# One-core convolution-attention kernel: the bias summed from two weighted records, block differences ahead of the statistics

## The reference

```python
qkv = jnp.einsum('bhwc,cd->bhwd', x, W_qkv)          # x here is _gn(x)
q, k, v = jnp.split(qkv, 3, axis=-1)                 # each turned to (b, c, n), n = h*w
k = jax.nn.softmax(k, axis=-1)
context = jnp.einsum('bdn,ben->bde', k, v)
out = jnp.einsum('bde,bdn->ben', context, q)         # back to (b, h, w, c)
return jnp.einsum('bhwc,cd->bhwd', out, W_out) + b_out
...
x = x + _L0_conv_ref(_gn(x), L0_conv_W_qkv, L0_conv_W_out, L0_conv_b_out)
```

## Time and profile before

| what | value |
|---|---|
| median of 3 runs | 1212.08 us (1211.97 to 1212.63) |
| the profiled execution | 1211.11 us, of which the span from first to last instruction is 1209.4 us |
| mean granted TensorE clock | 0.997 |
| TensorE matmuls, weight loads | 97% and 91% of the span |
| VectorE, ScalarE, GpSimd | 78%, 69%, 51% |
| DMA | 221 GB/s, 63% of the engines' time |

### The profile page before, as it was taken

The page is one execution under the profiler, slowest core; times in us unless marked ns, Lnnn a source line. Parts: engine busy times, 40 slices in busy tenths (PEclk is TensorE's granted clock), DMA queues, the critical chain, the costliest instruction groups (busy, mean ns, idle before and its releaser), DMA issues.

```text
span 1209.4 us, 21532 instructions
## 1 busy us (share of the span) xinstructions
PE 1174.3 (97%) x8270; PEld 1098.7 (91%) x8270; DVE 946.0 (78%) x1992; ACT 839.3 (69%) x1146; POOL 620.9 (51%) x289
## 2 busy tenths in 40 slices
PE   4989999999999999999999999999999999999998
PEld 3889998989999998999989999899899989999997
DVE  6978869788797877969788797887978778697571
ACT  5666757677686776857767676775867768577764
POOL 7645553655636356553655636456463564536520
PEclk9989999999999999999999999999999999999999
DMA  8438666486665767657486664866657576573524
GB/s 325 162 123 296 228 208 242 156 301 236 226 223 190 274 209 277 218 189 274 158 312 226 212 235 169 299 219 234 217 190 271 205 278 227 191 261 123 192 76 168
DMA packets 107078, 266.70 MB, mean 221 GB/s; under 512 B 10208, under 2 KB 10208, under 8 KB 106976
## 3 DMA queue, kind: packets, MB, share of 16 engines
q1 hardware_dynamic: 106976, 265.33, 63.1%
HBM read 198.18 MB, written 67.11 MB: 219 GB/s over the span
## 4 chain that ended last, share of the span: by engine, by line
PE 68%; DVE 16%; ACT 5%; POOL 5%; DMA 3%; issue 2%; SPq 0%; DVEq 0%; POOLq 0%; ACTq 0%
PE ps_k L446 23%; PE ps_e L612 16%; PE ps_e L621 8%; PE ps_e L528 5%; PE ps_e L540 5%; PE ps_e L530 5%; DVE dm L1025 3%; DMA xs<-in_xt_dram 3%; POOL x_lo L389 3%; DVE mx L981 3%; DVE e_raw L1041 2%; POOL rstd L399 2%; ACT e_raw L748 2%; DVE e_lo L1048 2%; ACT o_stage L782 1%
## 5 line engine op out<-in xcount | busy, mean ns | idle before, releaser
L383 POOL TENSOR_TENSOR xt_lo<-xt_raw,xt_hi 128x1024 fp32r<-128x1024 f32 x128 | 307.4, 2404 | 464.3 <-ACT xt_hi L725 194.2
L389 POOL TENSOR_TENSOR x_lo<-x_raw,x_hi 128x1024 fp32r<-128x1024 f32 x128 | 279.8, 2207 | 51.9 <-ACT x_hi L730 42.3
L981 DVE TENSOR_TENSOR mx<-ps_k,mx 128x256 f32<-128x256 f32 x480 | 203.3, 424 | 85.9 <-ACT e_raw L734 64.9
L782 ACT ACTIVATE o_stage<-ps_e,bias 128x512 f32<-128x512 f32 x253 | 170.9, 689 | 105.9 <-PE ps_e L621 105.8
L446 PE MATMUL ps_k<-wk_hi,xt_hi 128*128 128x256 f32 x1024 | 205.7, 283 | 0.4 <-DVE mx L981 0.2
L446 PE MATMUL ps_k<-wk_lo,xt_hi 128*128 128x256 f32 x1024 | 205.5, 283 | 0.0
L734 ACT ACTIVATE e_raw<-ps_k 128x512 f32<-128x512 f32 x256 | 141.4, 596 | 82.1 <-PE ps_k L446 82.1
L742 ACT ACTIVATE e_hi<-e_raw 128x1024 fp32r<-128x1024 f32 x128 | 134.9, 1054 | 65.9 <-DVE e_raw L1041 43.7
L446 PEld LDWEIGHTS ps_k<-wk_hi,xt_hi 128*128 128x128 f32 x1024 | 164.3, 189 | 9.5 <-issue 1.3
L909 DVE BATCH_NORM_STATS2 bn<-xs 128x6 f32<-128x512 f32 x240 | 154.1, 685 | 23.8 <-DMA xs<-in_xt_dram 22.4
L446 PEld LDWEIGHTS ps_k<-wk_lo,xt_hi 128*128 128x128 f32 x1024 | 157.7, 189 | 0.0
(11 more groups left out here) (145 smaller groups left out, 2056.7 us busy)
## 6 DMA issues: line engine op xcount, KB each, us to landing
xt_raw<-in_xt_dram SPq DMA_DIRECT2D x128, 512.0 KB, 4.4
x_raw<-in_xn_dram SPq DMA_DIRECT2D x128, 512.0 KB, 3.4
out_dram<-o_stage SPq DMA_DIRECT2D x127, 512.0 KB, 4.5
xs<-in_xt_dram SPq DMA_DIRECT2D x240, 256.0 KB, 5.0
w_setup<-in_w_dram SPq DMA_DIRECT2D x2, 256.0 KB, 9.8
out_dram<-o_stage SPq DMA_DIRECT2D x2, 256.0 KB, 2.0
wk<-in_w_dram SPq DMA_DIRECT2D x1, 256.0 KB, 10.2
wq_t<-in_w_dram SPq DMA_DIRECT2D x1, 256.0 KB, 11.4
```

The source lines that it names most:

```text
L383: nc.gpsimd.tensor_tensor(xt_lo[:, s], xt_raw[:, s], xt_hi[:, s].bitcast(F32), ALU.subtract).then_inc(xt_lo_ready, 1)
L389: nc.gpsimd.tensor_tensor(x_lo[:, s], x_raw[:, s], x_hi[:, s, :, 0:C].bitcast(F32), ALU.subtract).then_inc(x_lo_ready, 1)
L782: nc.scalar.activation(o_stage[:, u % O_SLOTS, h, :], src, ACT.Identity, bias=bias[:, h:h + 1]).then_inc(o_ready, 1)
L981: nc.vector.tensor_tensor(mx[:], tile, mx[:], ALU.max).then_inc(max_done, 1)
```

## The change

The bias is computed another way. GpSimd multiplies `neg_mean` with `rstd` (`scale_mean`, right behind each `rstd_of`). VectorE, behind `m_lo`, weights the two halves of the raw combined matrix in `ps_g0` with it and adds them (`bias_terms`, two records of 256 columns, in memory of `acc`), and TensorE sums that over the partitions with a column of ones: two products in place of four. `mean_bias` is gone, and `bias_of` adds `b_out` itself. In the emission, TensorE runs both halves of `emit_high` first, then `emit_low` of half 0, the bias, and `emit_low` of half 1. On VectorE the key maximum of chunk 1, half 0 moves between `bias_terms` and `bias_of`.

In the gathers of images 1 to 15, `block_scales` comes ahead of `mean_of`. GpSimd waits at the start of each period, that of image 0 included, for `dm_ready` in place of `diag_ready`.

```diff
+            def scale_mean(b, parity):
+                pool.wait_ge(rstd_ready, b + 1)
+                pool.wait_ge(mean_read, b + 1)
+                nc.gpsimd.tensor_tensor(scaled_mean[:, parity], neg_mean[:, parity], rstd[:, parity],
+                                        ALU.mult).then_inc(scaled_mean_ready, 1)
...
                 if more and b:
                     pool.wait_ge(var_parts_ready, n)
-                pool.wait_ge(diag_ready, b * 2 + 2)
+                pool.wait_ge(dm_ready, b + 1)
                 if more:
                     xt_low(n, np_, 0)
                     if b:
                         rstd_of(n, np_)
+                        scale_mean(n, np_)
                 for j in range(HALF, NCH):
                     x_low(b, j)
...
-            def bias_sum(b, parity):
-                pe.wait_ge(m_full_ready, b + 1)
+            def bias_sum(b):
+                pe.wait_ge(b_terms_ready, b + 1)
                 for h in range(CB):
-                    for c in range(CB):
-                        last = nc.tensor.matmul(ps_g0[:, 0, h:h + 1], m_full[:, c, h * P:(h + 1) * P],
-                                                neg_mean[:, parity, c:c + 1], start=(h == 0 and c == 0),
-                                                stop=(c == CB - 1), skip_group_check=True)
+                    last = nc.tensor.matmul(ps_g0[:, 0, h:h + 1], b_terms[:, h * P:(h + 1) * P], one_col[:],
+                                            start=(h == 0), stop=True, skip_group_check=True)
                 last.then_inc(bias_ps, 1)
...
                 emit_high(b, parity, 0, 0)
-                bias_sum(b, parity)
+                emit_high(b, parity, 0, 1)
                 emit_low(b, parity, 0, 0)
-                emit_high(b, parity, 0, 1)
+                bias_sum(b)
                 emit_low(b, parity, 0, 1)
...
+            def bias_terms(b, parity):
+                dve.wait_ge(scaled_mean_ready, b + 1)
+                dve.wait_ge(m_lo_ready, b + 1)
+                nc.vector.tensor_scalar(b_terms, ps_g0[:, 0, 0:C], scaled_mean[:, parity, 0:1], None,
+                                        ALU.mult).then_inc(b_first_ready, 1)
+                dve.wait_ge(b_first_ready, b + 1)
+                nc.vector.scalar_tensor_tensor(out=b_terms, in0=ps_g0[:, 1, 0:C], scalar=scaled_mean[:, parity, 1:2],
+                                               in1=b_terms, op0=ALU.mult, op1=ALU.add).then_inc(b_terms_ready, 1)
...
                 block_max(b, 1)
                 block_diag(b, 1)
+                block_scales(b)
                 if more:
                     mean_of(n, np_)
-                block_scales(b)
-                mean_bias(b, parity)
                 shift(b, 4)
...
                 take_m(b, parity)
+                bias_terms(b, parity)
+                if more:
+                    key_max(n, 1, 0)
                 bias_of(b)
                 if not more:
                     return
-                key_maxes(n, 1)
+                key_max(n, 1, 1)
```

More of the change, by code:

```diff
@@ L110, in build @@
         m_full = acc
+        b_terms = acc[:, 0, :]
         acc_hi = sb("acc_hi", [P, CB, C], F32R)
@@ L146, in build @@
         rz = sb("rz", [P, CB])
-        b_mean = sb("b_mean", [P, CB])
+        scaled_mean = sb("scaled_mean", [P, 2, CB])
         bias = sb("bias", [P, CB])
@@ L232, in build @@
         m_lo_ready = sem("m_lo_ready")
-        b_mean_ready = sem("b_mean_ready")
+        scaled_mean_ready = sem("scaled_mean_ready")
+        b_first_ready = sem("b_first_ready")
+        b_terms_ready = sem("b_terms_ready")
         bias_ps = sem("bias_ps")
@@ L404, in _ @@
             pool.wait_ge(wk_ready, 1)
+            scale_mean(0, 0)
             for j in range(5, NCH):
@@ L1080, in acc_low @@
                                                    op1=ALU.subtract).then_inc(acc_lo_ready, 1)
-            def mean_bias(b, parity):
-                if b == 0:
-                    dve.wait_ge(b_loaded, 16)
-                nc.vector.tensor_tensor(b_mean[:], b_col[:], neg_mean[:, parity, :],
-                                        ALU.subtract).then_inc(b_mean_ready, 1)
+            def bias_terms(b, parity):
[6 more added lines that the diff above has]
+                                               in1=b_terms, op0=ALU.mult, op1=ALU.add).then_inc(b_terms_ready, 1)
             def take_u(b, parity):
@@ L1121, in bias_of @@
                 dve.wait_ge(bias_ps, b + 1)
-                dve.wait_ge(b_mean_ready, b + 1)
-                if not (isinstance(b, int) and b == 0):
+                if b == 0:
+                    dve.wait_ge(b_loaded, 16)
+                else:
                     dve.wait_ge(o_ready, b * (CB * NCH))
-                nc.vector.tensor_tensor(bias[:], ps_g0[:, 0, 0:CB], b_mean[:], ALU.add).then_inc(bias_ready, 1)
+                nc.vector.tensor_tensor(bias[:], ps_g0[:, 0, 0:CB], b_col[:], ALU.add).then_inc(bias_ready, 1)
             for j in range(NCH):
@@ L1159, in first_gather @@
                 block_scales(0)
-                mean_bias(0, 0)
                 bn_half(1, 12)
```

## The result

The changed kernel takes 1200.31 us (median of 4 runs, 1197.77 to 1202.58), the kernel before in runs beside it 1212.36 us. The ratio is 0.9899, 95% interval 0.9878 to 0.992: 1.0% faster. The forecast was 1196.0 us with a range of 1192 to 1202.5; the time lies in the range, 4.3 us above the forecast. The profiled execution is the slowest of the four, 1202.58 us with a span of 1200.6.

What follows compares the result with a forecast made beforehand. TensorE, busy 97% of the span, was taken as the bound. 7.0 - 1.3 + 8.8 + 1.7 = 16.2 us off the profiled 1211.11 is 1194.9; with the median 0.97 above, 1196 us, range 1192 to 1202.5.

Steps and rivals of the forecast that it cites:

- The bias saves nothing: Rival: TensorE waits 0.44 us for the bias terms, or the removed matmuls were nearly free; 1201.6 us, chance 7%.
- scaled_mean: GpSimd's 2-column product ahead of `x_lo`: takes 0.4 us, bounds 0.3 and 0.71, leaving `x_lo` a 0.15 us margin.
- Four bias matmuls less: TensorE's emission: four records fewer at 0.11 us each, 0.44 us an image, 7.0 us in 16 images.
- later terms: TensorE's emission: VectorE's bias operand comes 0.08 us late an image, -1.3 us in 16 images.
- VectorE in the emission: VectorE gets 0.95 us more work in the emission, covered by waiting and idle time: cost nothing.
- The block differences first: Gather: `dm` no longer held, `e_lo` held instead, TensorE's wait for `x_lo` gone: 0.63 us in 14 images, 8.8 us.
- GpSimd keeps its turn: Rival: in the gather GpSimd's queued operations run before VectorE's waiting `e_lo`; slower, 1217.4 us, chance 5%.
- The wait moves and stays: Rival: in the gather `x_lo` of chunk 4 is as late as before; 1204.7 us, chance 8%.
- Image 0: First image's gather: `dm` is no longer held and `e_lo` of chunk 3 runs earlier; 1.7 us gained, bounds 0 and 4.

Runs made afterwards that it cites:

- bias_only: Changed kernel with the old gather order (statistics ahead of block differences, GpSimd waiting for `diag_ready`): 1208.27 us, ratio 0.9971 to the kernel before.
- bias_last: Changed kernel with TensorE's bias products moved behind `emit_low` of half 1: 1199.57 us, ratio 0.9902 to the kernel before.
- pe_old_order: Changed kernel with TensorE's two bias products back between `emit_high` and `emit_low` of half 0: 1220.31 us, ratio 1.0089 to the kernel before.
- order_only: Kernel before with only the new gather order and the wait for `dm_ready`, bias unchanged: 1202.44 us, ratio 0.993 to the kernel before.
- gate0_diag: Changed kernel with GpSimd waiting for `diag_ready` again in image 0 only: 1199.41 us, ratio 0.9905 to the kernel before.

## Why the prediction was right, and where 4 us stayed

The time alone does not single out the forecast: 1200.31 us lies 4.3 above 1196 and 1.3 below the 1201.6 of "The bias saves nothing". The traces do, since each step forecast for an undisturbed image is in them. The range held in part by luck. Its upper side had been made for late terms, a slow `scaled_mean` and an image 0 without gain, and none of these came; the shortfall that came had no term in the sum, and happened to be smaller than that allowance.

**Four bias matmuls less, 0.44 us, and later terms, 0.08 us.** Together 0.36 us an image was forecast, 0.42 is in the emission. The row of 0.11 us a record was the right price. An estimate from the 25 ns that the Trainium skill gives for an isolated small matmul (TensorE: Matmul & The Clock Gate, § Back-to-back issue gap) would be 0.1 us an image; the trace has four times that. "The bias saves nothing" falls by the emission of 3.26 us for 3.68, and by `bias_only`, faster by 0.29%. The terms were ready where they were forecast: 451.11 is 2.18 us after the emission's first product (448.93), for 2.13 to 2.27 worked out ahead (456.88 to 457.02 against 454.75). The waiting that this gives falls in a weight load and costs nothing that `bias_last` could show, so of the -1.3 us in the sum at most 0.3 were there (0.44 less 0.42, 16 times). `pe_old_order` shows the cover that the step rests on.

**VectorE in the emission at nothing.** No row of TensorE's waits speaks against it in undisturbed images, and the emission became as short as the bias alone makes it. In disturbed ones the copy of ScalarE is what TensorE waits for, but behind a late `xs`, not behind the bias.

**The block differences first, 0.63 us in 14 images.** 0.58 is in `order_only`, and in the changed kernel the wait for `x_lo` is gone from images 1 to 11. Every step is in the rows: `dm` 0.16, `e_lo` held (1.62 us, forecast 1.6 to 2.2), `rstd` behind it. "GpSimd keeps its turn" is refuted in both places. In the gather of image 5 `e_lo` ran as soon as `xt_lo` ended, and in image 0, where GpSimd had the next instruction waiting, `e_lo` ended at 60.59 and that instruction, `x_lo`, took 3.20 us for 2.20: it was the one held. What the Trainium skill says of two such instructions (SBUF — State Buffer, § Who interferes with whom) agrees, with 1.62, 1.68 and 3.20 us here. Who gets its turn when GpSimd's operation ends is seen at these two places of the program only, in 14 gathers at the one and once at the other.

**`scaled_mean`, 0.4 us with bounds of 0.3 and 0.71.** It has 0.195: the forecast was twice that, and the row lies below my lower bound, a straight line through 512 and 1024 columns. The estimate from the rate in the Trainium skill's GPSIMD Engine Reference, § 3.1, was under 0.1 us; the row lies about halfway between that and the line. The margin was 0.45 us, not 0.15: 0.2 of the difference is `scaled_mean`, and the rest mainly that `e_lo` ended 1.07 us after `xt_lo` and not 1.22. "The wait moves and stays" did not come about in this way.

**Image 0, 1.7 us.** 2.3 in the trace of the changed kernel from `dm` to `rz`, 1.3 in three others; at the end likely 1.5, not settled.

**The sum.** Without disturbances the traces give 14 x 1.01 = 14.1 us, 2.3 for image 0 and 0.4 for the last image, less 0.3 in what follows its `rz`: 16.5 us (15.7 with 0.95 us an image), and 16.2 were forecast. What was missing is a term for transfers. An image that is 1.0 us shorter has the same bytes to move, and the lateness of GpSimd had covered late loads of `x_raw`. The second is in the rows of images 11 to 14, 3.4 us; the first is argued from the half-output runs. Together they give back 7.0 us in the profiled execution, the longest of its four, and 1.4 in that of `gate0_diag` (5.6 - 4.2). In the first, 16.5 - 7.0, less 0.7 us by which image 0's `dm` happened to come later, is 8.8 us, the difference of the spans. With half the output 2.6 us are given back, and the gain there is 13.7 us. The medians with full output, 12.0 us, stand between. The forecast had no price for a transfer that lands late. "The wait moves and stays" came true in a small part: images 12 to 14 wait for `x_lo`, through `x_raw`.

**Left open.** Which property makes those loads late, the rate of all transfers together or the moment at which SyncE comes to issue them. Halving the output changes both, and the two tries at SyncE's order moved the lateness about. More slots for `xs`, which would let SyncE issue earlier, were not tried. Why the loads of `x_raw` are late in the last four images above all is open too. No version that writes the whole output beat the changed kernel by more than the intervals.

## What to carry to other kernels

When two engines wait for each other, look for a short instruction that shows the duration of a long one on the other engine (2.40 us for a kind that takes 0.16), and ask which instruction will stand in its place once it is moved. Move the instruction that uses a new operand back by as many matmuls as its producer needs, and check that cover by taking it away. And when a steady wait is removed on a kernel that moves much data, price what the wait had hidden: compare the waits for transfers, and the spread between images, before counting on the full sum.

## What was not expected of the hardware

A GpSimd product of 128x2 took 0.195 us each of 16 times, while `rstd`, a power of the same shape, has 0.71 where nothing stands beside it. In a row their pace is 1.10 / 4 = 0.275 us. Leaving out 33 of 267 MB of transfers took 4 to 5 us off a kernel whose TensorE is busy for 97% of the span, and 5 to 7 off the faster one.
